# A block with routed experts: loading the down weights and the last eight experts' gate and up weights after the dispatch

## What is computed

```python
x = x + ga * attention(h)
h = layernorm(x) * (1 + cb) + sb
# six of 32 experts for each token, by sigmoid scores in groups
g = jnp.einsum('th,ehm->etm', xf, gate_w)      # gate_w, up_w: (32, 256, 176)
u = jnp.einsum('th,ehm->etm', xf, up_w)
eo = jnp.einsum('etm,emh->eth', silu(g) * u, down_w)   # down_w: (32, 176, 256)
routed = jnp.einsum('te,eth->th', combine, eo)
shared = silu(xf @ sh_gate_w) * (xf @ sh_up_w) @ sh_down_w
x = x + gb * (routed + shared)
```

## Time and profile before

| | us |
|---|---|
| median of 3 timed runs | 537.88 (537.27 to 538.41) |
| the profiled execution, first to last instruction | 580.9 |
| PE busy in it | 470.8 (81%) |
| POOL busy in it | 288.1 (50%) |
| first block turned by PE (L1438) | at 279.39 |

### The profile page before, as it was taken

The page is one execution under the profiler, slowest core; times in us unless marked ns, Lnnn a source line. Parts: engine busy times, 40 slices in busy tenths (PEclk is TensorE's granted clock), DMA queues, the critical chain, the costliest instruction groups (busy, mean ns, idle before and its releaser), DMA issues.

```text
span 580.9 us, 9471 instructions
## 1 busy us (share of the span) xinstructions
PE 470.8 (81%) x1994; PEld 324.4 (56%) x1995; DVE 225.1 (39%) x971; ACT 176.4 (30%) x429; POOL 288.1 (50%) x257
## 2 busy tenths in 40 slices
PE   4898989728787509759699999999999999999700
PEld 4455656317546205335477777777777777777500
DVE  2726788205872106301233333333333333333203
ACT  2231331202221003002144444444444444444300
POOL 2303513760777742750065566655665666655540
PEclk9999987977896859959799999999999999999955
DMA  8999111330458852932266677567666767666478
GB/s 284 341 339 386 53 42 46 125 113 0 153 133 266 286 191 80 315 140 72 61 98 104 102 118 109 94 107 105 114 105 101 111 104 110 107 112 102 50 216 238
DMA packets 86193, 83.25 MB, mean 143 GB/s; under 512 B 22329, under 2 KB 80155, under 8 KB 86172
## 3 DMA queue, kind: packets, MB, share of 16 engines
q1 hardware_dynamic: 63708, 50.49, 29.9%
q0 software_dynamic: 20160, 30.43, 28.6%
q10 hardware_dynamic: 2304, 2.10, 1.1%
HBM read 43.13 MB, written 40.90 MB: 145 GB/s over the span
## 4 chain that ended last, share of the span: by engine, by line
PE 68%; another core or an unknown queue 10%; issue 8%; DMA 5%; DVE 4%; ACT 3%; POOL 1%; SPq 0%; ACTq 0%; POOLq 0%
PE bank L1445 21%; PE bank L1460 15%; PE bank L1362 5%; PE bank L1262 5%; PE bank L1438 4%; PE bank L1453 4%; PE bank L1248 3%; DMA gate_up<-token_sums 2%; PE bank L1373 2%; PE bank L1164 2%; DMA token_sums<-tok_buf,dest 2%; PE bank L1335 1%; DMA XH<-in_L_attn_x 1%; PE bank L1196 1%
## 5 line engine op out<-in xcount | busy, mean ns | idle before, releaser
L587 POOL DMA_INDIRECT token_sums<-tok_buf,dest x104 | 161.4, 1552 | 136.0 <-ACT tok_buf L777 56.7
L1445 PE MATMUL bank<-gate_up,tok_buf 128*128 x416 | 142.1, 464 | 0.4 <-DVE tok_buf L1111 0.4
L559 POOL DMA_INDIRECT pair_rows<-XH,rows_i x96 | 95.3, 992 | 59.1 <-DVE rows_i L1030 30.6
L1111 DVE COPY tok_buf<-bank 128x256 f32<-128x256 f32 x104 | 44.2, 425 | 177.7 <-PE bank L1438 172.3
L1460 PE MATMUL bank<-down,tok_buf 88*128 x416 | 109.0, 384 | 0.0
L1445 PEld LDWEIGHTS bank<-gate_up,tok_buf 128*128 128x128 f32 x416 | 79.8, 192 | 29.3 <-issue 2.1
L1460 PEld LDWEIGHTS bank<-down,tok_buf 88*128 88x128 f32 x416 | 70.6, 190 | 7.6 <-issue 0.2
L777 ACT ACTIVATE tok_buf<-bank,tok_buf 128x256 f32<-128x256 f32 x104 | 49.2, 473 | 53.1 <-PE bank L1460 31.0
L1362 PE MATMUL bank<-tok_buf,sh_gu 128*128 128x512 f32 (+1 forms) x96 | 48.6, 659 | 19.8 <-ACT sh_rows L722 13.5
L762 ACT ACTIVATE tok_buf<-bank 128x176 f32<-128x176 f32 x104 | 33.0, 317 | 80.8 <-PE bank L1445 76.7
L1438 PEld LDWEIGHTS bank<-ident,tok_buf 128*128 128x128 f32 x208 | 27.4, 142 | 38.2 <-issue 29.9
(11 more groups left out here) (153 smaller groups left out, 465.6 us busy)
## 6 DMA issues: line engine op xcount, KB each, us to landing
tok_buf<-pair_rows SPq DMA_DIRECT2D x104, 128.0 KB
gate_up<-in_L_ffn_gate_w SPq DMA_DIRECT2D x8, 704.0 KB, 8.5
gate_up<-in_L_ffn_up_w SPq DMA_DIRECT2D x8, 704.0 KB, 8.7
down<-in_L_ffn_down_w SPq DMA_DIRECT2D x2, 2816.0 KB
pair_rows<-sh_rows SPq DMA_DIRECT2D x1, 5120.0 KB, 19.2
XH<-in_L_attn_x SPq DMA_DIRECT2D x4, 512.0 KB, 9.7
token_sums<-sh_rows ACTq DMA_DIRECT2D x16, 128.0 KB
gate_up<-token_sums SPq DMA_DIRECT2D x4, 512.0 KB, 5.6
```

The lines of the kernel that those rows point to most:

```text
L559: nc.gpsimd.indirect_dma_start(out=pair_rows, out_offset=bass.IndirectOffsetOnAxis(ap=rows_i[:, t, k:k + 1], axis=0), in_=XH[:, t, :], in_ ...
L587: nc.gpsimd.indirect_dma_start(out=token_sums[c % 2], out_offset=bass.IndirectOffsetOnAxis(ap=dest[:, c:c + 1], axis=0), in_=yw[:, c, :], ...
L1111: V.tensor_copy(xT[:, c % 2], banks[0][:, 0:C].rearrange("p (k n) -> p k n", k=KC)).then_inc(xT_copied, 1)
L1445: last = mm(banks[1 + c % 2][:, 0:M2], xT[:, c % 2, k, :], gate_up[:, bass.ds(e * (KC * M2) + k * M2, M2)], start=k == 0, stop=k == KC - 1)
```

## The change

On SP, the loads of the first four blocks' rows, with the waits ahead of them, are put in front of the six weight loads. The waits themselves stay, and so does PE's wait for `ld_late`.

```diff
             sp.wait_ge(h2_ready, NT)
             sp.wait_ge(gb_stored, 16)
+            SP = mybir.EngineType.SP
+            sp.wait_ge(recs_ready, 2 * B)
+            sp.wait_ge(mapf_ready, 1)
+            await_read(sp, ("map",))
+            sp.wait_ge(dispatched, 16 * NT * TOPK)
+
+            def load_rows(c, col):
+                sp.dma_start(xg[:, c, :], pair_rows[bass.DynSlice(col, P, E), 0:C]).then_inc(x_loaded[c], 16)
...
+            cols = load_values(sp, SP, 1, 0, 0)
+            for c in range(R):
+                load_rows(c, cols[c])
+
             for m in range(2):
                 sp.dma_start(dn_v[0:KD, m, :].rearrange("p (e c) -> p e c", e=E),
                              down_w[:, m * KD:(m + 1) * KD, :].rearrange("e p c -> p e c")).then_inc(ld_late, 16)
-
-            SP = mybir.EngineType.SP
-            sp.wait_ge(recs_ready, 2 * B)
-            sp.wait_ge(mapf_ready, 1)
             load_gate_up(EARLY, E, ld_late)
-
-            await_read(sp, ("map",))
-            sp.wait_ge(dispatched, 16 * NT * TOPK)
...
-            cols = load_values(sp, SP, 1, 0, 0)
-            for c in range(R):
-                load_rows(c, cols[c])
```

More of the change, by code:

```diff
@@ L436, in _ @@
             sp.wait_ge(gb_stored, 16)
-            for m in range(2):
-                sp.dma_start(dn_v[0:KD, m, :].rearrange("p (e c) -> p e c", e=E),
-                             down_w[:, m * KD:(m + 1) * KD, :].rearrange("e p c -> p e c")).then_inc(ld_late, 16)
             SP = mybir.EngineType.SP
@@ L443, in _ @@
             sp.wait_ge(mapf_ready, 1)
-            load_gate_up(EARLY, E, ld_late)
             await_read(sp, ("map",))
@@ L457, in _ @@
                 load_rows(c, cols[c])
+            for m in range(2):
+                sp.dma_start(dn_v[0:KD, m, :].rearrange("p (e c) -> p e c", e=E),
+                             down_w[:, m * KD:(m + 1) * KD, :].rearrange("e p c -> p e c")).then_inc(ld_late, 16)
+            load_gate_up(EARLY, E, ld_late)
             def step(turn, last):
```

## The result

The changed kernel takes 592.82 us (590.89 to 595.08, 4 runs), the kernel before on the same chip 538.14 us: a ratio of 1.1027, with a 95% interval of 1.099 to 1.1063. That is 54.7 us more. The forecast was 569.4 us with a range up to 584; its direction was right, its size was not. The rival that was priced nearest is the one called slower still, 589 us. After the change all of the kernel's text stands one line earlier, so that the blocks' first turn, L1438 before, is L1437.

What follows compares the result with a forecast made beforehand. The prediction took the landed dispatch, paced by POOL's issues, to set the PE-bound loop's start. Row loads to 263.6, weights 32.7 and registers 3.0 gave +35.0 us, less 3.5 for PE's tail: 569.4 us, range 546 to 584.

Steps and rivals of the forecast that it cites:

- slower still: Rival for the uncovered weights: 140 GB/s is the down load's own rate, weights take 52.4 us, +51.2 us, 589 us; 6%.
- The reading of the profile: Before the block loop: in timed runs the loop begins when the dispatch, POOL issuing one DMA after another, has landed.
- PE's tail: Before the loop: PE's shared expert ends 15.1 us after the rows in the profile, at most 7.1 us in timed runs.
- Part 1: On SP: row loads put before the weights still wait for the dispatch and start no earlier; gain nothing.
- Part 2: Dispatch stretch: six weight DMAs leave it, but POOL's issues, 1.26 us apart, set the pace; the dispatch gains nothing.
- a dispatch that ends much before 257 us: Sign in the profile after: it would say that the first profile's waits are real in timed runs too.
- Part 3: Behind the rows: six weight DMAs, 8.65 MB, come with nothing to hide them while PE waits at `ld_late`; 32.7 us.
- The term of 32.7 us: Uncovered weights before the loop: 21.5 us down at 269 GB/s, 8.5 us gate and up, 2.7 us to the last landing.
- the bound of 52.4: Upper bound in us for the uncovered weights, with the down load at the 140 GB/s seen beside the dispatch.
- Part 4: On PE: register loads, so far under the wait for rows, come behind `ld_late`; 2.96 us.
- The sum: Loop's first turn at 299.3 instead of 264.3, +35.0 us, less 3.5 us for PE's tail: +31.5 us, 569.4 us.
- the likeliest case: The forecast's own case: weights uncovered before a loop that begins with the dispatch; 569 us, range 561 to 581, 70%.

Runs made afterwards that it cites:

- the second profile: The kernel before, profiled again with nothing edited: 538.94 us, with a span of 537.2 us.
- the first profile: The kernel before, unedited, as profiled for the forecast: a span of 580.9 us, against a timed median of 537.88 us.
- the load of 80 partitions: The larger piece in the changed kernel with each down load cut into 80 and 8 partitions: 584.87 us, 1.0898 times before.

## Why the prediction was wrong

*The reading of the profile was right.* In timed runs the loop begins when the dispatch has landed: the second profile shows it at 234.31, and the register loads taken out of that chain shorten the kernel. Of the 7.1 us that were left for PE's tail nothing was there: PE was done before the dispatch.

*Part 1, the row loads gain nothing: right.* The first is issued at 231.35 in the changed kernel and at 232.13 in the second profile of before, 2.15 and 2.14 us after the dispatch has landed.

*Part 2, the dispatch gains nothing: right.* It lands at 229.20 after the change and at 229.99 in the second profile of before, and POOL's issues are 1.26 to 1.27 us apart in both. The prediction took a dispatch that ends much before 257 us for a sign against it. The dispatch did end some 30 us earlier, but in the kernel before as well; it was the first profile that stood apart. PE's shared expert did gain, 217.74 against 219.72 us, and that was cover under the dispatch. ACT's stores gained most: ACT waited 20.5 us for them in the second profile of before, and 3.7 us after the change. POOL's pace, 1.26 to 1.27 us from issue to issue, did not suffer by the down load.

*Part 3, the weights come uncovered: right in kind, wrong in size, and this is the step that failed.* It put the down load at 269 GB/s, "if alone it can draw what all drew", because "the 140 were clearly shared with a busy queue". Alone it ran at 138. The term of 32.7 us measured 52.7; the bound of 52.4, at the rate seen, was the answer, and I gave it 6%. On the 11 engines of my estimate the load's 77.0% of 16 is 112%, and the load of 80 partitions shows 112.0% of 16. If it is 11, the engines in use always had a packet under way, and a share under 100% was no sign of a rate that the load could still gain.

*Part 4, PE's register loads behind the wait: right,* 2.32 us for 2.96.

*The sum* took 3.5 us off for a tail of PE that the timed run doesn't have. With the measured terms it is 31.5 + (52.7 − 32.7) + (2.3 − 3.0) + 3.5 = 54.3 us; 54.7 were measured. One bound was off in itself: half way from 32.7 to 52.4 us of weights is 42.6 and not 41, which would make the likeliest case end at 583 and not at 581 us.

*Why the rate is 138* is shown in part. It is not the number of engines, and which partitions a load covers decides. That the writing into the SBUF holds it up, and not the rows in DRAM that go with the partitions, is the likelier reading, as other rows in DRAM with the same partitions ran at 142 GB/s, and not shown. By what mechanism the partitions set the rate, no run shows.

## What to carry to other kernels

The share of the DMA engines doesn't say how fast a load could be: 43.6% beside the dispatch and 77.0% alone went with about the same rate, and 112% or 113% went with 208 GB/s in one load and with 339 in another. Price a load at the rate seen for it, not at the share that others leave free. Before a transfer is moved out of the way of others, ask what sets the pace there; the dispatch here, paced by its issuing engine at 1.26 to 1.27 us an issue, gained nothing from emptier DMA engines, and the transfer lost its cover. When a profiled execution is far off the timed ones, take a second one of the same kernel: here it settled what the reading of the first could only argue.

## What the runs showed of the hardware

Loads of 1 KB rows into the SBUF ran at 65, 138, 183 and 205 to 208 GB/s for the same weights, depending on which partitions a DMA covered: 8 in a row, 88, 8 at a distance of 4, and 64 to 80. A packet took 139 ns with 8 in a row, 91 ns with 88 partitions and 45 ns with 8 at a distance of 4, but 16 x 5 x 1.12 / 1014 = 88 ns with 80: its time gives the rate only together with the share, which was 56.5%, 77.0%, 52.3% and 112.0%. And one profiled execution of a kernel ran 43 us longer than its timed runs, with waits that no recorded work explains, which a second profile of it did not show.
